# Mixture fit with repeated TensorE products inside its two waits for VectorE

## What is computed

```python
# data: (8 samples, 4096 positions, 8 features), N = 2 components, EM_ITERS = 10
for _ in range(EM_ITERS):
    diff2 = ((data[:, :, None, :] - mu[:, None, :, :]) ** 2 / var[:, None, :, :]).sum(-1)
    logdet = jnp.log(var).sum(-1)
    logp = -0.5 * (diff2 + logdet[:, None, :] + k * log2pi) + jnp.log(wts)[:, None, :]
    resp = jax.nn.softmax(logp, axis=2)
    Nk = resp.sum(1)
    mu = jnp.einsum('bpn,bpk->bnk', resp, data) / Nk[..., None]
    ex2 = jnp.einsum('bpn,bpk->bnk', resp, data ** 2) / Nk[..., None]
    var = jnp.maximum(ex2 - mu ** 2 + EPS, EPS)
    wts = Nk / P
```

## Time and profile before

| | us |
|---|---|
| median of 3 runs | 3862.01 |
| lowest and highest | 3856.91, 3864.22 |
| the profiled execution, its own time | 3863.4 |
| its span, first to last instruction | 3861.8 |
| TensorE busy in the span | 3209.1 (83%) |
| VectorE busy | 3018.2 (78%) |
| ScalarE busy | 1871.3 (48%) |
| mean granted clock of TensorE | 0.919 |

### The profile page before, as it was taken

How to read it: one execution, slowest core, us unless ns; L and a number is a source line. 1 busy time by engine, 2 the same in 40 slices (tenths; PEclk the granted TensorE clock), 3 DMA queues, 4 the chain that set the end, 5 groups by cost and what they waited for, 6 DMA issues and landing times. The chain is left out here.

```text
span 3861.8 us, 68816 instructions
## 1 busy us (share of the span) xinstructions
PE 3209.1 (83%) x23738; PEld 2390.1 (62%) x23738; DVE 3018.2 (78%) x3491; ACT 1871.3 (48%) x4272; POOL 645.3 (17%) x325
## 2 busy tenths in 40 slices
PE   7999999999999745998556887888889887888877
PEld 3454554545455345776334787877778787877777
DVE  5999999999999933113443897979889797979877
ACT  4555555555555310222221555555655556555654
POOL 0000000000000000000000333333333333333333
PEclk9999999999999865998666999999999999999999
DMA  6646556556556212221002899999999999999998
GB/s 275 254 201 259 243 206 264 231 219 264 220 231 265 116 73 98 102 116 44 0 0 78 289 345 322 348 327 346 346 340 343 326 343 337 343 325 347 353 349 305
DMA packets 348925, 945.54 MB, mean 245 GB/s; under 512 B 25937, under 2 KB 58833, under 8 KB 329490
## 3 DMA queue, kind: packets, MB, share of 16 engines
q1 hardware_dynamic: 339346, 907.41, 63.3%
q0 software_dynamic: 9216, 33.56, 2.1%
HBM read 638.90 MB, written 301.99 MB: 244 GB/s over the span
## 5 line engine op out<-in xcount | busy, mean ns | idle before, releaser
L189 DVE SCALAR_TENSOR_TENSOR first_acc<-first_x,first_wd,first_acc 128x1024 f32<-128x1024 f32 (+1 forms) x1088 | 1297.8, 1275 | 57.4 <-ACT first_acc L214 46.0
L1172 PE MATMUL second_o<-second_right,second_left 128*128 128x128 f32 x8192 | 1106.9, 286 | 186.5 <-POOL second_left L964 121.1
L1172 PEld LDWEIGHTS second_o<-second_right,second_left 128*128 128x128 f32 x8192 | 1023.0, 200 | 239.7 <-issue 211.2
L964 POOL TENSOR_TENSOR second_left<-second_mid_copy,second_coef_rep 64x1024 f32<-64x1024 f32 x256 | 610.6, 2385 | 1881.9 <-ACT second_mid_copy L1278 1876.4
L1417 DVE SCALAR_TENSOR_TENSOR second_x<-second_o,second_shift,second_x 128x512 f32<-128x512 f32 x1024 | 734.1, 738 | 233.5 <-PE second_o L1172 231.1
L218 ACT ACTIVATE first_xT<-first_tp 128x512 f32<-128x512 f32 x1024 | 608.3, 597 | 533.6 <-PE first_tp L244 533.0
L244 PE MATMUL first_tp<-all_const,first_x 128*128 128x128 f32 x4096 | 679.4, 291 | 79.8 <-issue 41.5
L244 PEld LDWEIGHTS first_tp<-all_const,first_x 128*128 128x128 f32 x4096 | 441.3, 143 | 461.1 <-issue 444.4
L256 PE MATMUL first_freq<-first_xT,all_p 128*64 128x256 f32 x4096 | 667.4, 407 | 17.7 <-ACT first_xT L218 8.1
L1257 ACT ACTIVATE second_mid<-second_dd,all_inter 128x128 f32<-128x128 f32 x1024 | 327.1, 390 | 386.0 <-DVE second_mid L1399 374.7
L256 PEld LDWEIGHTS first_freq<-first_xT,all_p 128*64 128x64 f32 x4096 | 210.6, 136 | 193.9 <-issue 178.8
(11 more groups left out here) (215 smaller groups left out, 2327.3 us busy)
## 6 DMA issues: line engine op xcount, KB each, us to landing
second_x<-in_x SPq DMA_DIRECT2D x512, 512.0 KB, 7.5
out<-second_x SPq DMA_DIRECT2D x512, 512.0 KB, 5.7
first_x<-in_x SPq DMA_DIRECT2D x48, 4224.0 KB, 25.3
first_x<-in_x SPq DMA_DIRECT2D x16, 4096.0 KB
second_dd<-downsampled SPq DMA_DIRECT2D x112, 384.0 KB, 6.4
downsampled<-first_acc POOLq DMA_DIRECT2D x64, 512.0 KB, 11.6
average_xd<-downsampled SPq DMA_DIRECT2D x16, 2048.0 KB, 8.4
second_dd<-downsampled SPq DMA_DIRECT2D x16, 320.0 KB, 6.2
```

The lines of the kernel that those rows point to most:

```text
L189: nc.vector.scalar_tensor_tensor(out=acc[c][:, :, left:], in0=tap_window(xt[c], (s, dh, dw), OUT1), scalar=wd[:, t, k:k + 1], in1=acc[c][: ...
L964: return eng.tensor_tensor(left[a][rows, odd:HALF:2, :, :].rearrange("p n (t s) g -> p n t s g", t=T), turned[rows, :, :, :].unsqueeze(3). ...
L1172: last = nc.tensor.matmul(ob[n][:, r, :], left[a][:, r, n, :], right[a][:, r, :], start=True, stop=True)
```

## The change

TensorE's program in the loop gets a helper that multiplies the ones by the first 512 columns of `ft` into `tp[1]`, as often as it is told. It is called for two products behind `parameters` and for six behind the transposes L676. The products carry no semaphore, and nobody reads their result.

```diff
+                def keep_running(times):
+
+                    for _ in range(times):
+                        nc.tensor.matmul(tp[1][:, :, :].rearrange("p j k -> p (j k)"), k("ones"),
+                                         ft[:, 0:4, :].rearrange("p n k -> p (n k)"), start=True, stop=True)
+
                 pe.wait_ge(copied, groups)
                 with pe.Fori(0, ITERS) as i:
                     parameters(pe, i)
+                    keep_running(2)
                     pe.wait_ge(weights, i + 1)
                     for h in range(2):
                         for j in range(4):
@@
                     last.then_inc(scores, 1)
+                    keep_running(6)
                     pe.wait_ge(resps, i + 1)
```

## The result

Over six runs of each, the changed kernel takes a median of 3831.9 us (3821.3 to 3834.2) and the kernel before 3860.0 us (3847.4 to 3865.2). The ratio is 0.992, with a 95% interval of 0.991 to 0.994: 28 us less, 0.8%. The forecast was 3828 in a range of 3821 to 3848. The profiled execution of the changed kernel took 3834.2 us, with a span of 3832.5 and a mean granted clock of 0.934 (before: 0.919).

The account below looks back on a forecast made before the run. The fit's loop was taken as bound by a chain between engines, its long blocks at 1.2 GHz. 17.5 + 9 x 14.70 = 149.8 us instead of 183.6 gave 3828 us; own spread 3821 to 3837, range 3821 to 3848.

Parts of the forecast that it names:

- What bounds the loop, the chain: Fit's loop: each iteration is one chain hopping between engines, nothing long overlapping, 18.4 us an iteration.
- The price of a product at the high clock: Added 128x512 products: 0.44 us a record, two records each; 1.77 us for two products, 5.31 for six.
- They fit: Both waits at the high clock: two products end 0.3 us before L667, six end 0.6 before L684; cost nothing.
- L674 and L692 at 1.85 us: The loop's two long TensorE blocks, L667 and L684 before the change: 1.85 us each instead of 3.57.
- Rival B: L684 does not double in pace, staying at 3.14 us: 1.3 us an iteration back, 3841 us; chance 0.04.
- The count of records in 0.2 us: L684 shows 12 records in 0.2 us at the low clock, 16 after a rise; read as doubled pace.
- The clock stays high: Through the changed loop the clock holds 1.00, its longest stretch without a large product being 1.7 us.
- The first iteration, 17.5 us: Loop's first iteration starts at the low clock: 4.45 us for L631 to L667 and 2.7 for L667.
- All of it moves up: Everything behind the loop begins after it ends, so the whole 33.8 us gain reaches the kernel's time.
- Rival A: Clock falls once or twice an iteration of the loop, 1.4 us for one fall: 3842 or 3853 us; chance 0.15.
- Rival C: The six softmax products run at the low clock every iteration and hold L684 back: 3896 us; chance 0.05.
- Rival D: Loop's clock goes on swinging, gains in L667 and L684 cancelling losses at added products: 3862 us; chance 0.06.

Follow-up runs that it names:

- e4: The changed kernel with ten added products in the softmax instead of six; loop 176.6 us, where the changed kernel takes 149.5.
- e6: The changed kernel with six transposes in the place of each added product (12 and 36 of them); loop 149.1 us.
- e10: The changed kernel with one product behind the parameters instead of two, and six in the softmax; loop 157.1 us.
- e9: The changed kernel plus added products in the k-means loop, the fit's end and the second pass's first part, there also behind each transpose group; 3805.8 us.
- e1: The changed kernel without the six products in the softmax, only the two behind the parameters; loop 183.5 us.
- e2: The changed kernel without the two products behind the parameters, only the six in the softmax; loop 167.8 us.
- e11: The changed kernel with two products behind the parameters and three in the softmax instead of six; loop 187.7 us.
- e3: The changed kernel with the same number of added products, but 16 columns wide instead of 512; loop 183.7 us.
- e5: The changed kernel with one product behind the parameters and three in the softmax, half of each; loop 169.8 us.
- e8: The changed kernel plus added products in the k-means loop, the fit's end and the second pass's first part, none between its transposes; 3803.3 us.

## Why the prediction was right

- *What bounds the loop, the chain:* right. It was read from rows that name VectorE as the releaser of both blocks, and the pieces that belong to VectorE are unchanged in the profile after: 2.51 and 6.45 us against the 2.50 and 6.44 of the earlier trace rows.
- *The price of a product at the high clock, 0.44 a record:* 0.434 in e4. At the low clock, 0.89 estimated: the first two products of the changed kernel take 3.69 us for four records, 0.92.
- *They fit:* right, with 0.08 and 0.64 us to spare. Forecast were 0.3 and 0.6. The first was a closer thing than I had it, since L663 starts 0.47 us after L631, about as counted, and the last record ends only at 2.43 instead of 2.2.
- *L674 and L692 at 1.85 us:* 1.86 and 1.88. Rival B falls with that. The count of records in 0.2 us was the right row to weigh against the 3.14 us. The Trainium skill's 62 ns for each matmul without hardware decode ("TensorE: Matmul & The Clock Gate", Part 1) does not bind here: 64 records in 1.88 us are 29 ns each.
- *The clock stays high:* right, but its reasons don't carry it, and that part was in some measure luck. I counted the transposes as pause because of a row at 0.50; e6 shows that transposes back to back hold the clock alone. The other, that 1.7 us is shorter than the pauses of rows 8, was right for the outcome, yet the longest pause isn't the measure: e10 has the same 1.7 us and the clock falls in six of nine iterations. And the averaging stage, which was taken to be at 1.00 as a whole, is so only from about 1539 us on in the kernel before. The earlier trace rows shows 1600 to 1700; from 1525.8 to 1538.0 TensorE is busy for 12.20 of 12.20 us at 0.50.
- *The first iteration, 17.5 us:* it took 16.81. L631 to L674 was 4.57 (4.45 counted), but L674 took 1.86, not 2.7: the clock rose as it began, not halfway in it. This is the one term of the loop that was clearly mis-sized, by 0.8 us. The sum came out at 149.5 against 149.8.
- *All of it moves up:* 34.1 us less in the loop (33.8 forecast), 29.3 in the span. The missing 4.8 us lie ahead of the loop and in the main part of the second pass, which transfers fill. That part took 1735 us here, 1745 in e9, and 1728 to 1739 in the other kernels. I had this in the range (3821 to 3837) and not in the sum, rightly: nothing tells beforehand which way it goes.
- *Rival A* was priced at 1.4 us for a fall, with part of the low stretch hidden in the slack of the two products. e10 has 1.45, with the low stretch in L674 alone, so the near agreement is partly chance.
- *Rival C* doesn't happen with 2 and 6. Its mechanism does, in e1, e2 and e11, and in e11 it makes the loop slower than with no products at all (187.7 us against 183.6). It was the right rival to fear, with a wrong trigger: it comes with too few products, not with the pause at L680.
- *Rival D*, no change at all, is the outcome of e3, but not by its mechanism: there no block gains and none loses.

## What to carry to other kernels

- Where TensorE's blocks stand on a chain and the granted clock over the stage is between 0.50 and 1.00, price each block at both levels; the difference, summed over the chain, is what unread products in the waits can bring. Those that did it here were wide or came back to back (e3's narrow ones, which left the wait empty, did nothing). They write where nobody reads and stand behind the increment that starts the other engine.
- Fill the wait nearly to its end, and fill every wait of the loop. Half of the cover brought 0 to 16 of 34 us (e1, e2, e5), or a loss (e11), because products that start at the low clock cost double and delay the block that they were to help. Past the gap each costs its full time (e4).
- Measure the stage and the total. The shorter fit was seen in the total (29 of 34 us), though the main part behind it has a DMA share of 0.95; the 17 us of e9, from the start of that same pass, were seen in part in one execution and not in the medians.
- Take a gain for shown only where the edit is. The averaging stage rises to the high clock after 4 to 25 us in these kernels, which moves the total by several us with no edit near it.

## What the runs showed of the hardware

- A record that counts as busy doesn't by itself raise the clock. The row of e8 has 20.00 of 20 us busy at 0.50 (64-row tiles with one 128-row product among them), that of e1 in the averaging stage 20.00 of 20 at 0.50 (128-row tiles, transposes and products of 64 columns), and e3 has 116 of 175 us busy at 0.62, more than the 99 of 183.5 before, with the loop no shorter. The Trainium skill ("TensorE: Matmul & The Clock Gate", Part 1) says that the clock follows how busy the engine has been, and that activity releases the throttle; by the busy share of the profile, these rows disagree with it, so that share doesn't tell which clock is granted.
- The moment of the rise differs between executions with the same work: 5.8 to 25.0 us from the start of the averaging stage in the kernels that have nothing changed ahead of it.
- Where the clock is restored, small operations gain too: L683 0.66 instead of 1.12 us, the k-means block 1.06 instead of 1.87.
- Inside a loop the clock's swings can repeat. In e1 and e11 the iterations fall into fixed patterns to 0.1 us (18.4, 16.6, 19.6; 17.7, 19.9), so a loop can lock into a bad one; in e5 and e10 they don't.
